# Expert attention on one core: order of a unit's transposes on TensorE, and place of a PSUM copy among ScalarE's exponentials

## What is computed

```
for e in range(4):                                   # experts
    q = (x @ wq[e].T).reshape(b, s, 12, 16).transpose(0, 2, 1, 3)
    k, v = ...                                       # the same with wk[e], wv[e]
    scores = einsum('bhqd,bhkd->bhqk', q, k) / sqrt(16)
    scores = where(mask, scores, -1e30)              # a window of 64 tokens back
    attn = softmax(scores, axis=-1)
    outs.append(einsum('bhqk,bhkd->bhqd', attn, v) ... @ wo[e].T)
fused = concatenate(outs, axis=-1)
return silu(fused @ w_gate.T) * (fused @ w_up.T)
```

## Time and profile before

| | before |
|---|---|
| median of 3 runs | 1119.93 us (1117.1 to 1120.66) |
| the profiled execution, its own time | 1116.88 us |
| its span, first to last instruction | 1115.2 us |
| granted TensorE clock, mean | 0.999 of 2.4 GHz |
| PE, PEld busy over the span | 1068.7 us, 863.9 us |
| ACT, DVE, POOL busy over the span | 768.1 us, 722.6 us, 571.1 us |

### The profile page before, as it was taken

One profiled execution on the slowest core, in us unless ns is written; L12 is line 12 of the kernel. 1 busy time (PEld: TensorE's weight loads), 2 busy tenths in 40 slices (PEclk: granted clock), 3 DMA queues, 4 the chain that ended last, 5 costly groups with the idle time before them and its releaser, 6 DMA issues.

```text
span 1115.2 us, 34039 instructions
## 1 busy us (share of the span) xinstructions
PE 1068.7 (96%) x13103; PEld 863.9 (77%) x13103; DVE 722.6 (65%) x2240; ACT 768.1 (69%) x3370; POOL 571.1 (51%) x859
## 2 busy tenths in 40 slices
PE   6999998999998999999999999999999999999998
PEld 4789886777776465368888888888888888887677
DVE  8566566676666115457878787887778787877201
ACT  2356547777776345458898888888888888888231
POOL 2256667444544866536565545555564655455200
PEclk9999999999999999999999999999999999999999
DMA  8100603000000000010000000000000000000000
GB/s 272 30 4 11 126 7 74 2 2 2 2 2 1 1 1 1 1 52 2 2 3 2 3 3 2 3 3 2 3 3 2 3 2 3 3 2 3 11 22 32
DMA packets 35057, 19.66 MB, mean 18 GB/s; under 512 B 24657, under 2 KB 32337, under 8 KB 34897
## 3 DMA queue, kind: packets, MB, share of 16 engines
q1 hardware_dynamic: 34752, 17.00, 5.8%
q10 hardware_dynamic: 144, 0.49, 0.2%
HBM read 14.93 MB, written 1.77 MB: 15 GB/s over the span
## 4 chain that ended last, share of the span: by engine, by line
PE 71%; ACT 17%; DVE 9%; issue 1%; POOL 1%; DVEq 0%; POOLq 0%
ACT e_W L1947 12%; PE banks L1821 6%; PE banks L1532 5%; PE banks L1809 4%; PE banks L1750 4%; PE banks L2199 3%; PE banks L2153 3%; PE banks L1837 3%; PE banks L1758 3%; PE banks L1258 2%; PE banks L1856 2%; PE banks L505 2%; PE banks L1861 2%; PE banks L1279 2%; PE banks L1797 2%; ACT e_WT L1953 2%
## 5 line engine op out<-in xcount | busy, mean ns | idle before, releaser
L2120 POOL TENSOR_TENSOR e_W<-e_W,e_RS 128x384 f32<-128x384 f32 x256 | 205.8, 828 | 243.3 <-DVE e_RS L1997 240.5
L1947 ACT ACTIVATE e_W<-banks,e_MX 128x128 f32<-128x128 f32 x768 | 270.1, 371 | 14.4 <-DVE e_MX L1983 12.2
L1947 ACT ACTIVATION_READ_ACCUMULATOR e_W<-banks,e_MX 128x1 f32 x768 | 161.0, 210 | 0.0
L1821 PE MATMUL banks<-ident,e_W 128*128 128x128 f32 x768 | 111.5, 275 | 8.2 <-DVE e_ON L2022 5.3
L1750 PE MATMUL banks<-XT,e_wqk 64*128 64x141 f32 x744 | 119.1, 295 | 0.0
L1758 PE MATMUL banks<-e_wv,XT 128*128 128x192 f32 (+3 forms) x512 | 109.9, 344 | 0.6 <-DVE e_PT L2001 0.6
L1750 PEld LDWEIGHTS banks<-XT,e_wqk 64*128 64x128 f32 x744 | 96.4, 188 | 18.0 <-issue 16.6
L1941 ACT COPY e_PT<-banks 128x512 f32<-128x512 f32 x128 | 71.8, 587 | 46.6 <-PE banks L1821 46.2
L1506 POOL TENSOR_TENSOR f_W<-f_W,e_RS 128x423 f32<-128x423 f32 x64 | 56.3, 892 | 86.8 <-DVE e_RST L1485 76.5
L1821 PEld LDWEIGHTS banks<-ident,e_W 128*128 128x128 f32 x768 | 86.7, 143 | 15.9 <-DVE e_ON L2022 13.8
L1983 DVE TENSOR_REDUCE e_MX<-banks 128x3 f32<-128x384 f32 x128 | 65.4, 552 | 37.5 <-PE banks L1809 37.5
(11 more groups left out here) (328 smaller groups left out, 2713.3 us busy)
## 6 DMA issues: line engine op xcount, KB each, us to landing
xp<-in_patches_dram SPq DMA_DIRECT2D x4, 768.0 KB, 9.3
H<-in_h_dram SPq DMA_DIRECT2D x1, 1728.0 KB, 13.1
out_dram<-H SPq DMA_DIRECT2D x6, 288.0 KB, 2.3
m_hid<-in_e_gu_dram SPq DMA_DIRECT2D x1, 1536.0 KB, 8.8
m_hid<-in_e_o_dram SPq DMA_DIRECT2D x4, 192.0 KB, 6.8
e_wqk<-in_e_qk_dram SPq DMA_DIRECT2D x8, 96.0 KB, 2.4
e_wqk<-in_e_qk_dram SPq DMA_DIRECT2D x24, 32.0 KB, 2.4
tokw<-in_tok_w_dram SPq DMA_DIRECT2D x1, 576.0 KB, 5.1
```

Of the source, the lines that this page charges most:

```text
L1821: tr = nc.tensor.transpose(dst[:, (t % 4) * P:(t % 4 + 1) * P], W[n % 2][:, t, :], ident[:, :])
L1947: ex = nc.scalar.activation(W[n % 2][:, t, :], bank[i][:, x * P:(x + 1) * P], ACT.Exp, bias=MX[:, t:t + 1], accum_out=SM[n % 2][:, t:t + 1])
L2120: nc.gpsimd.tensor_tensor(x, x, RS[n % 2][:, 3 * i:3 * i + 3].unsqueeze(2).broadcast_to([P, 3, P]), ALU.mult).then_inc(s_nm, 1)
```

## The change

In PE's turn n, `scores(n)` stood behind the transposes of sets 0 and 1 of unit n-1; it now stands between them. `out_project(n - 2)` stood behind the transposes of the tail; it now stands in front of them. In ACT's turn n, the copies of sets 0 and 1 stood together in front of `expert_k(n + 1)`; the copy of set 1 now stands behind the first three of the unit's exponentials. No instruction is added or left out, and DVE, POOL and SP are as before.

```
@@ tensor
                             transpose(n - 1, 0)
+                        if n < N:
+                            scores(n)
+                        if 1 <= n <= N:
                             if n >= 2:
                                 pe.wait_ge(s_o, 2 * n - 2)
                             pe.wait_ge(s_nm, 5 * n - 2)
                             transpose(n - 1, 1)
-                        if n < N:
-                            scores(n)
-                        if 1 <= n <= N:
                             pe.wait_ge(s_pa, 2 * n - 1)
                             pe.wait_ge(s_nm, 5 * n - 1)
                             transpose(n - 1, 2)
+                        if n >= 2:
+                            out_project(n - 2)
+                        if 1 <= n <= N:
                             pe.wait_ge(s_pa, 2 * n)
                             pe.wait_ge(s_nm, 5 * n)
                             transpose_tail(n - 1)
-                        if n >= 2:
-                            out_project(n - 2)
                         if n < N:
                             project_v_and_qk(n)
@@ scalar
                         if 1 <= n <= N:
                             evacuate_weights(n - 1, 0)
-                            evacuate_weights(n - 1, 1)
                         if n + 1 < N:
                             expert_k(act, n + 1, bank[6])
                         if n < N:
                             exponentials(n, 0)
+                        if 1 <= n <= N:
+                            evacuate_weights(n - 1, 1)
+                        if n < N:
                             exponentials(n, 1)
                             exponentials(n, 2)
                             exponentials(n, 3)
```

## The result

| | before | changed |
|---|---|---|
| median of 14 runs each | 1120.3 us | 1124.84 us |
| lowest to highest | 1117.1 to 1125.29 | 1123.25 to 1133.52 |
| ratio of the changed kernel | | 1.0054, 95% interval 1.0032 to 1.0076 |
| the profiled execution, its own time; span | 1116.88; 1115.2 | 1130.49; 1128.8 |
| granted TensorE clock in it, mean | 0.999 | 0.992 |

The sign was right and the median lies in the range, near its lower end, but the forecast size was more than double the measured one.

What follows compares the result with a forecast made beforehand. The k copies' chain, behind expert_q, attended copies and reciprocal L2080, was taken to set the exponentials' start; start gains against 0.54 us per copy made 63 intervals total 549.2 us against 535.3, +14 us, so 1134, range 1124 to 1147.

Steps and rivals of the forecast that it cites:

- What bounds: Expert stage: exponentials follow ACT's k copies, behind expert_q, attended copies and reciprocal L2080; k copies held about 60 times, not 30.
- turn A: Turn with R = 731.03: exponentials start at R + 3.17 instead of 3.30, gain 0.13; interval 8.72 us.
- Start of the exponentials: ACT's first exponential after the k copies: R + 3.17, 3.03 or 3.36 by kind of turn.
- R: Start of the tail's reciprocal L2080 on DVE, the mark from which turns are measured; intervals averaged 8.50 us before.
- B: Turn with R = 739.34, PE late before: start at R + 3.03 instead of 3.57, interval 8.58 as before.
- with a residual: Turn with R = 756.26, where DVE's additions come first: start at R + 3.36, interval 8.91 against 8.87 before.
- Price of the copy: Set 1's copy, uncovered in ACT's burst of exponentials: 0.54 us in each of 63 intervals, +34.0 us.
- lower bound for this price: The copy in ACT's burst would cost 0 if the burst had slack; its back-to-back rows were said to exclude that.
- PE in time: PE 0.2 to 0.3 us early; first maximum 0.35 us before k copies end; tail wait up to 0.9 us.
- Output projection: On PE, moved in front of the tail: order only, fills part of PE's new wait, cost nothing.
- Slower still: Rival, chance 0.20: DVE falls behind, L2080 slips and PE's scores pass; 1146 us; decided where DVE stops waiting before L2080.
- The equal case: Rival, chance 0.08: in all turns the exponentials' start gains 0.54 us, which eats the copy; 1120 us.

Runs made afterwards that it cites:

- doubled copy: The changed kernel with the copy of set 1 made twice in the burst, the first into an unused buffer: 1155.84 us.
- DVE edit: DVE's attended copies moved in front of the tail's reciprocal: in the changed kernel 1124.88 us, in the kernel before 1115.93 us.

## Why the prediction was right or wrong

- *What bounds.* Right: the k copies' chain ended only 0.13 us before the scores' in turn A, and with the scores sooner it set nearly every turn: 62 waits of the k copies (forecast: about 60), hardly a wait for the maxima (2.5 us in three turns). Where the k copies are missing, in the last interval, the start came 1.02 us sooner; the sum had counted that interval as 8.72, and it was 7.76.
- *Start of the exponentials.* Right: R + 3.20 in the third turn, of A's kind (761.92 after 758.72), against 3.17, R + 3.02 against 3.03 in B, 8.74 - 5.43 = 3.31 against 3.36 with a residual.
- *Price of the copy.* This term of the sum failed, by its size: "ACT runs its fourteen exponentials back to back" and so +0.54 us in each of 63 turns. The burst grew from 5.01 to 5.43 us, by 0.42. Two parts: the copy costs 0.50 and not half of the pair's 1.07 (burst of 5.43 against 4.93 in the kernel with the scores alone, 746.83 to 751.76, which has neither copy nor pause; 0.49 by the doubled copy). The pair's merged row is about one step of 0.48 from start to start and one whole row of 0.59, and its half is neither. And the burst before was not back to back: its third group waited for the last maxima. In the kernel before, between the sixth and the seventh exponential,

```profile
727.75 0.38 ACT L1947 ACTIVATE e_W<-banks,e_MX 128x128 f32<-128x128 f32 x1
...
727.85 0.31 DVE L1992 TENSOR_REDUCE e_MXT<-banks 104x2 f32<-104x152 f32 x1
...
728.19 0.37 ACT L1947 ACTIVATE e_W<-banks,e_MX 128x128 f32<-128x128 f32 x1
```

  0.44 us lie between the starts instead of 0.34. The third group waits in the code until all four maxima are counted (`s_mx` at 4n + 4); the tail's, L1992, end at 728.16, and it starts at 728.19. The maxima that it reads are the third count; a kernel that waits for three was not tried. The pause costs 0.08 (5.01 against 4.93), and the copy, which makes the burst later, swallows it. 63 x 0.12 = 7.6 us too much, which takes the forecast of 14 to 6. The prediction's lower bound for this price, "its back-to-back rows exclude that", leaned on the same reading: the burst had 0.08 us of slack.
- *PE in time.* Right in the outcome, with less room than forecast: PE was to be 0.2 to 0.3 us early, but the maxima waited for its scores 33 times (0.21 us in turn B, 752.51), and only because the k copies ended later still did it cost nothing. The wait at the tail was 0.6 us by PE's weight loads (0.4 by its matmuls) in turns with the short output projection, where 0.9 was the forecast's upper end, and 0.2 in 17 of the others.
- *Output projection.* Nothing by itself (1119.88), right; but "cost nothing" hides that it is a condition: without it the other two moves cost 63 us.
- *Rivals.* Slower still did not come: in the gate's turn L2083 had no wait left (758.72), the sign that the rival named, but it still started 0.03 us after the last exponential's rows end (758.69), and the turn was 8.45. The rule of the Trainium skill (Perfetto Trace Analysis, Optimization Strategy) that the gaps of the most contended engine should be closed named the right wait, but this case does not bear out that closing it makes the kernel faster: 12.8 of PE's 13.3 us were closed, and the kernel is slower.
- *The equal case* would have needed the start of the exponentials to gain in each turn what B gained. It did not; but with B's 0.55 against a copy of 0.42, B alone is now 0.13 us shorter (8.45 for 8.58).
- *Open:* whether the change makes the clock fall more often. It was full in seven of its 14 runs and in none of the four of the variant with the copy behind the k copies, whose turns are the same; of the kernel before 37 runs beside the variants have their clock on record, two at 0.999 and the others lower. The fall near 500 us is in the profiled runs of the changed kernel, of the scores alone, of the copy behind the k copies and of both kernels with the DVE edit, and not in that of the doubled copy, which has all three moves. PE's waits in front of that place are alike with the fall and without it: 0.94 and 0.80 us in the changed kernel, 0.93 and 0.79 in the kernel before, 0.94 and 0.79 with the doubled copy. So it follows neither the moves nor these waits. No kernel was made to tell what lowers it.

## What to carry to other kernels

A wait on the busiest engine is worth only what the second chain into the same point leaves: measure that chain from a common mark before moving the wait. Here a copy that fitted into an engine's wait was free there and cost nearly its full length at both places tried behind the instructions that end the wait. Moves must be priced together: the scores alone cost 50 us, the copy alone 80, both without the output projection 63, all three 6. And a burst should be read start by start before it is called back to back. Where one reciprocal in a queue holds several chains, move what stands behind it without need: that one edit gave 6 us where the three moves lost 6.

## What was not expected of the hardware

The 128x512 copy took 0.50 us of ACT's time inside a run of exponentials and 0.48 in front of it (750.05 to 750.53), though its own row says 0.59 (a row's duration is not what it takes from its engine); two in a row took 1.07. And at the full clock the changed kernel repeats within a few tenths of a microsecond (1123.25 to 1123.80 in seven runs; at a mean of 0.998 the kernel before spreads over 1.6, 1119.2 to 1120.8), while stretches at 1.2 GHz in single executions moved it by up to 10 us, among them one in a stage that both kernels share: a profile must be compared with the clock beside it, turn by turn, and not by its span.
